# A chain of eight transformer stages on one core: each next stage's first statistics, normalizing and quantizing ahead of the last update of x

## What is computed

```
x = x + att0(layernorm(x), ctx)     # one head of 512, softmax, keys and values are the context and x itself
x = x + ffn0(layernorm(x))          # activations quantized to 8 bits per token, ternary weights, sigmoid gate
x = x + att1(layernorm(x), ctx)     # 16 heads, 4 key heads, rms norm and rotation of q and k, causal part
x = x + ffn1(layernorm(x))          # as ffn0, with silu and a Walsh-Hadamard transform of the hidden layer
x = x + att2(layernorm(x), ctx)     # linear attention with a gate
x = x + layer(layernorm(x))         # one ternary 512x512 product and a bias
x = x + att3(layernorm(x), ctx)     # x and output quantized to whole numbers, 16 heads of 32, softmax
x = x + ffn3(layernorm(x))          # weights interpolated (Catmull-Rom) from control points, silu gate
```

## Time and profile before

| | us |
|---|---|
| median of 3 runs | 2520.35 |
| lowest and highest run | 2519.28, 2526.17 |
| the profiled execution | 2523.76 |
| its span in the profile | 2521.9 |
| PE busy | 2291.3 (91%) |
| DVE busy | 1141.5 (45%) |
| ACT busy | 780.8 (31%) |
| POOL busy | 174.4 (7%) |

### The profile page before, as it was taken

How to read it: one execution, slowest core, us unless ns; L and a number is a source line. 1 busy time by engine, 2 the same in 40 slices (tenths; PEclk the granted TensorE clock), 3 DMA queues, 4 the chain that set the end, 5 groups by cost and what they waited for, 6 DMA issues and landing times.

```text
span 2521.9 us, 27455 instructions
## 1 busy us (share of the span) xinstructions
PE 2291.3 (91%) x10317; PEld 1328.8 (53%) x10340; DVE 1141.5 (45%) x2303; ACT 780.8 (31%) x1569; POOL 174.4 (7%) x356
## 2 busy tenths in 40 slices
PE   8998999999998969999999997968976888799999
PEld 3544544556664436666666664643433555444444
DVE  1432455364214835555555546844544666521111
ACT  1223322312222523333333324533332555311111
POOL 0000000000001211010010001100000000000000
PEclk9998999998999989999999999988988999899999
DMA  5442433434524210300000013010001111000000
GB/s 210 189 156 95 194 149 129 159 125 130 173 78 159 71 39 22 123 19 25 19 20 24 19 30 122 14 35 20 18 4 56 50 50 56 23 1 9 5 5 13
DMA packets 52519, 178.99 MB, mean 71 GB/s; under 512 B 5457, under 2 KB 25233, under 8 KB 46590
## 3 DMA queue, kind: packets, MB, share of 16 engines
q1 hardware_dynamic: 50662, 139.49, 16.1%
q0 software_dynamic: 1728, 37.75, 3.9%
HBM read 121.58 MB, written 46.47 MB: 67 GB/s over the span
## 4 chain that ended last, share of the span: by engine, by line
PE 72%; DVE 14%; ACT 6%; issue 5%; DMA 2%; POOL 1%; SPq 1%; DVEq 0%; ACTq 0%; POOLq 0%
PE psum L119 60%; PE psum L112 7%; PE psum L1438 4%; DVE small L2234 2%; DVE R L562 1%; ACT WK L2184 1%; ACT R L500 1%; PE psum L1040 1%; DVE R L1198 1%; DVE R L561 1%; PE psum L2152 1%; DVE R L1197 1%; DVE WK L242 1%; DVE small L1606 1%; DVE R L1755 0%
## 5 line engine op out<-in xcount | busy, mean ns | idle before, releaser
L119 PE MATMUL psum<-R,WK 128*125 128x512 f32 (+7 forms) x3458 | 1332.1, 531 | 30.0 <-DMA WK<-in_ctxT 7.4
L119 PEld LDWEIGHTS psum<-R,WK 128*112 128x112 f32 (+4 forms) x3472 | 583.2, 174 | 651.4 <-issue 531.1
L112 PE MATMUL psum<-small,WK 112*125 112x112 f32 (+6 forms) x2164 | 299.7, 269 | 150.2 <-ACT WK L2190 28.5
L112 PEld LDWEIGHTS psum<-small,WK 112*125 112x125 f32 (+6 forms) x2164 | 241.9, 155 | 252.4 <-issue 128.2
L119 PE MATMUL psum<-WK,R 128*112 128x375 f32 (+3 forms) x704 | 220.2, 451 | 13.1 <-DVE R L1755 8.9
L119 PE MATMUL psum<-WK 125*112 125x128 f32 (+3 forms) x1264 | 204.8, 299 | 1.5 <-DVE WK L890 1.2
L119 PEld LDWEIGHTS psum<-WK 125*112 125x112 f32 (+2 forms) x1264 | 165.7, 178 | 54.6 <-issue 43.7
L1606 DVE TENSOR_REDUCE small<-psum 112x1 f32<-112x487 f32 x128 | 84.9, 664 | 221.2 <-PE psum L119 219.4
L119 PE MATMUL psum<-R 128*128 128x112 f32 (+3 forms) x960 | 159.4, 310 | 28.0 <-DVE R L1755 22.8
L1528 ACT ACTIVATE WK<-psum,small 112x487 f32<-112x487 f32 x128 | 96.9, 757 | 259.1 <-DVE small L1608 258.4
L119 PEld LDWEIGHTS psum<-WK,R 128*112 128x112 f32 (+2 forms) x704 | 111.5, 170 | 86.7 <-issue 14.0
(11 more groups left out here) (212 smaller groups left out, 2041.2 us busy)
## 6 DMA issues: line engine op xcount, KB each, us to landing
R<-in_wf POOLq DMA_DIRECT2D x6, 4096.0 KB, 13.8
d_w<-R POOLq DMA_DIRECT2D x6, 2048.0 KB, 18.4
R<-d_w SPq DMA_DIRECT2D x6, 2048.0 KB, 14.7
WK<-in_ctxT SPq DMA_DIRECT2D x16, 750.0 KB, 5.5
d_v<-WK SPq DMA_DIRECT2D x16, 750.0 KB
R<-in_wq SPq DMA_DIRECT2D x7, 1024.0 KB, 7.7
R<-in_wo SPq DMA_DIRECT2D x6, 1024.0 KB, 16.7
d_k<-X SPq DMA_DIRECT2D x8, 750.0 KB, 3.2
```

The lines of the kernel that those rows point to most:

```text
L112: ins = pe.transpose(dst, src, idn[0:k, 0:k])
L119: ins = pe.matmul(dst, lhs, rhs, start=k == 0, stop=k == len(pairs) - 1)
```

## The change

`x_ready` loses its second form: it always waits for the last update, and it stands only where an engine touches what the old stage may still use. For PE that is behind the first transposes. ACT and POOL have none. Where x itself is needed, `x_back` waits for the copies of one batch.

Each stage has a new function `first(dve)`: the statistics, normalizing (and quantizing) of its first batch or tile, in the FFNs the statistics of the second tile too. The stage before calls it on DVE ahead of its own last update. `att1`'s tables are loaded at the start of `att0` and worked out there (`prepare`); `att2`'s bias and first two summaries are loaded with its weights during `att1` and `ffn1`; `layer`'s bias is loaded when `ffn1` is over; `att3`'s weights, biases and first keys and values are now all loaded when `att2` is over (the weights came sooner before). Tiles are placed so that these loads overwrite nothing.

```diff
         def x_ready(eng, n):
+            updates[n - 1].wait_drained(eng, TILES[n - 1] - 1, "y")
+
+        def x_back(eng, n, b=None):
             if n in (2, 4):
...
+                for i in range(NT):
+                    count = [at for at, _, _ in pieces(i)]
+                    if b is None or b in count:
+                        eng.wait_ge(sem(f"back{i}"), 16 * len(count) * (n // 2))
...
+        def ln_first(dve, n, xn, done):
+            x_back(dve, n, 0)
+            ln_stats(dve, dve_chain.on(dve), n, 0)
+            ln_apply(dve, n, 0, xn).then_inc(done, 1)
...
@@ context_part, dve @@
                         dve.tensor_reduce(wtot[:, b, 0:1], wsum[:, b, :], AX, ALU.add).then_inc(sem("context_sum"), 1)
+                        if b == 2:
+                            dve.wait_ge(sem("w2_threshold"), 1)
...
+                        elif b in (3, 4):
+                            quantize(dve, link, b - 3)
                         dve.wait_ge(sem("context_threshold"), b + 1)
...
@@ context_part, pool @@
                         pool.tensor_tensor(rk, ssp, neghalf[0:SP, :], ALU.pow).then_inc(sem("context_norms"), 1)
+                        if (b, s) == (2, 1):
+                            pool.wait_ge(sem("w2_abs"), 1)
+                            link(pool.partition_all_reduce(wtot[:, 6, 1:2], wsum[:, 6, 0:1], P, RADD))
...
-                    if b == 1:
-                        pool.wait_ge(sem("w2_abs"), 1)
...
@@ ternary_ffn @@
+            def first(dve):
+                stats(dve, 0)
+                quantize_x(dve, 0)
+                stats(dve, 1)
...
             def pe(pe):
-                x_ready(pe, n)
-                pe.wait_ge(sem(f"{stage}_weights"), 16 * (4 if hadamard else 3))
...
+                    for i, (b0, b1, b2, b3) in enumerate(iterations(4, NT)):
+                        if i == 2:
+                            x_ready(pe, n)
+                            pe.wait_ge(sem(f"{stage}_weights"), 16 * 3)
...
                         if b3 is not None:
+                            if b3 == NT - 1:
+                                stages[n + 1]["first"](dve)
                             update(b3)
...
@@ attention1 @@
             def sync(sp, load_next):
                 x_ready(sp, n)
+                x_back(sp, n)
...
@@ attention2, load @@
+                sp.dma_start(bg, io.bg2.to_broadcast([T, D])).then_inc(sem(f"{stage}_bias"), 16)
+                for b in range(2):
+                    load_kv(sp, b)
...
@@ attention3, dve @@
                         elif kind == "y":
                             out_ring.wait_filled(dve, b, "y")
+                            if b == NB - 1:
+                                stages[n + 1]["first"](dve)
                             link(dve.tensor_tensor(xr[:, b, :], xr[:, b, :], bp, ALU.add))
```

More of the change, by code:

```diff
@@ L201, in x_ready @@
         def x_ready(eng, n):
+            updates[n - 1].wait_drained(eng, TILES[n - 1] - 1, "y")
+        def x_back(eng, n, b=None):
             if n in (2, 4):
-                eng.wait_ge(sem(f"{'ffn0' if n == 2 else 'ffn1'}_back"), 16 * sum(len(list(pieces(i))) for i in range(NT)))
-            elif n:
-                updates[n - 1].wait_drained(eng, NB - 1, "y")
-            else:
-                raise ValueError(n)
+                for i in range(NT):
+                    count = [at for at, _, _ in pieces(i)]
+                    if b is None or b in count:
+                        eng.wait_ge(sem(f"back{i}"), 16 * len(count) * (n // 2))
         def context_stored(eng):
@@ L1244, in dve @@
                         if b3 is not None:
+                            if b3 == NT - 1:
+                                stages[n + 1]["first"](dve)
                             update(b3)
-                        if b0 is not None:
-                            quantize_x(b0)
+                        if b0:
+                            quantize_x(dve, b0)
                             if b0 + 1 < NT:
-                                stats(b0 + 1)
+                                stats(dve, b0 + 1)
                         if b2 is not None:
@@ L1285, in pool @@
                         h_scales(b2)
-            return dict(load=load, sync=sync, back=back, pe=pe, act=act, dve=dve, pool=pool)
+            return dict(load=load, sync=sync, back=back, first=first, pe=pe, act=act, dve=dve, pool=pool)
         def attention1(stage, n):
@@ L1301, in attention1 @@
             kTn = R.get(2 * NG * T, s=2, g=NG, t=T)
-            later = R.get(T, rows=T, dt=BF16)
+            later = Area(R1, 12160).get(T, rows=T, dt=BF16)
             W = Area(R0, 12288)
@@ L1558, in dve, with first @@
                     link(dve.tensor_tensor(c[:, 64:128], tmp[:, 64:128], cos, ALU.mult))
+            def first(dve):
+                ln_first(dve, n, xn, sem(f"{stage}_xn"))
+            def dve(dve):
+                x_ready(dve, n)
+                link = dve_chain.on(dve)
                 def four(v, a=0, z=P):
@@ L1935, in dve @@
                     if b3 is not None:
+                        if b3 == NB - 1:
+                            stages[n + 1]["first"](dve)
                         add_to_x(dve, dve_ring, b3)
@@ L2016, in dve @@
                     if b1 is not None:
+                        if b1 == 0:
+                            dve.wait_ge(sem(f"{stage}_bias"), 16)
+                        if b1 == NB - 1:
+                            stages[n + 1]["first"](dve)
                         link(dve.tensor_tensor(xr[:, b1, :], xr[:, b1, :], bias, ALU.add))
@@ L2099, in sync, with scale_of, normalized, whole_numbers @@
                                  ).then_inc(sem(f"{stage}_ctxV{b % 2}"), 16)
+            def scale_of(link, v, c):
+                dve = link.eng
+                link(dve.tensor_reduce(am, v, AX, ALU.max, apply_absolute_value=True))
+                link(dve.tensor_scalar(c, am, 1.0 / 127.0, 1e-8, ALU.mult, ALU.max))
+                link(dve.reciprocal(rr, c))
+                link(dve.tensor_scalar(v, v, rr, MAGIC, ALU.mult, ALU.add))
+            def normalized(dve, b):
+                link = dve_chain.on(dve)
+                link(ln_apply(dve, n, b, xn))
+                scale_of(link, xn, cx[:, b % 2:b % 2 + 1])
+            def whole_numbers(dve, b, name, v, vi):
+                if b:
+                    odd_ring.wait_filled(dve, b - 1, f"{name}T")
+                dve.tensor_scalar(vi, v, -MAGIC, 127.0, ALU.add, ALU.min).then_inc(sem(f"{stage}_{name}"), 1)
+            def first(dve):
+                ln_stats(dve, dve_chain.on(dve), n, 0)
+                normalized(dve, 0)
+                whole_numbers(dve, 0, "xi", xn, xi)
             def pe(pe):
-                x_ready(pe, n)
                 pe.wait_ge(sem(f"{stage}_weights"), 64)
@@ L2369, in act, with stats, first @@
                         drain(b0, "xnT", xnT)
+            def stats(dve, i):
+                dve.wait_ge(sem(f"{stage}_x{i % 2}"), arrived[i])
+                ln_stats(dve, dve_chain.on(dve), n, i, xf[i])
+            def first(dve):
+                stats(dve, 0)
+                ln_apply(dve, n, 0, xn, xf[0]).then_inc(sem(f"{stage}_xn"), 1)
             def dve(dve):
@@ L2434, in _ @@
                 if n == 4:
-                    x_ready(sp, n)
+                    stages[5]["load_bias"](sp)
                     spline["load"](sp)
-                stages[n]["sync"](sp)
+                if n == 6:
+                    x_ready(sp, n - 1)
+                    stages[n]["load"](sp)
+                if n != 5:
+                    stages[n]["sync"](sp)
             if upto < 8:
```

249 lines of the change are left out of this document (120 added, 129 removed).

## The result

| | before | changed |
|---|---|---|
| median of 4 runs, us | 2522.9 | 2440.58 |
| lowest and highest, us | 2519.28, 2526.17 | 2440.16, 2442.24 |
| the profiled execution, us | 2523.76 | 2440.16 |
| its span, us | 2521.9 | 2438.4 |

The ratio of the changed kernel to the one before is 0.9675, with a 95% interval from 0.9658 to 0.9692: 82 us or 3.3% less. The forecast was 2440.0 us. The two profiled executions lie 83.6 us apart, their spans 83.5.

A forecast was written before the change was run, and what follows sets the result against it. PE was taken to be busy nearly everywhere, so gains come only from its pauses and half clock. Terms summed to 80.3 us, taking the median from 2520.35 to 2440.0 us; range 2428 to 2460.

The forecast's parts named there:

- Prologue: Prologue: PE's 17.9 us wait behind POOL's W2 reduce and the quantizing waits go, with clock: 28.2 us, bounds 19.6 and 29.
- First FFN: Seam into the first FFN: DVE still waits for the copy of x, the last update follows; 0 us, bounds -1 and +1.
- Attention 1: Seam into attention 1: the 15.47 us pause goes, with half-clock loss; 18.6 us, first keys in time by 1.6 us.
- Attention 2: Seam into attention 2: pauses for x's way back and the bias go, 4.1 + 6.8 + 1.0 clock = 11.9 us.
- Layer, last FFN: Layer seam: only spline units' time remains, 3.9 us won. Last FFN seam: transposes sooner, product waits for update, 2.0 us won.
- Attention 3: Seam into attention 3: 1.1 us of the 8.8 us pause remain; 7.7 + 1.0 clock = 8.7 us, bounds 4 and 11.
- A stretched reduce: Prologue: quantizing beside POOL's all-reduce stretches it, so 5.8 and 2.8 us stay: 2448.6 us; 8%.
- `first` late at the second FFN and attention 3: At these two seams `first` is not reached before y is full; 4.6 us less won at each: 2449.2 us; 5%.
- First keys binding: Attention 1: first keys and values landing 7 us later cost 5.4 us: 2445.4 us; 5%.
- Seams that stay in part: Five later seams: waits the old barrier hid replace the pauses: 2473.6 us, or 2456.8 with half lost; 8%.
- More clock than counted: All seams win the 3.1 us of clock seen at attention 1: 2431.6 us; 9%.
- Slower by throttle: Long full stretches: without pauses the throttle grants less clock; 200 us more at half clock gives 2540 us; 2%.

The follow-up runs named there:

- The early copies: Changed kernel with the copies of the first FFN's tiles 0, 1 and 2 issued on SP ahead of the prologue's last four coefficient stores: 2432.18 us.
- the last FFN's early tile: Changed kernel with the last FFN's first statistics and normalizing ahead of the wait for attention 3's last y: 2437.25 us.
- the late order: Changed kernel with `first` put behind the last update of x on DVE again at all seven seams: 2464.5 us.
- the kernel with the barrier: Changed kernel with PE again waiting, from the first FFN on, for x's last update and all copies back at each stage's start: 2456.23 us.

## Why the prediction was right, point by point

| stretch | forecast | measured | of it pauses | of it clock |
|---|---|---|---|---|
| prologue | 28.2 | 30.6 | 25.0 | 5.6 |
| attention 0 | 0 | 2.7 | 0.0 | 2.7 |
| first FFN, from its seam | 0 | 1.7 | 1.1 | 0.6 |
| attention 1 | 18.6 | 18.8 | 15.4 | 3.4 |
| second FFN | 7.0 | 6.6 | 6.4 | 0.2 |
| attention 2 | 11.9 | 9.8 | 10.8 | -1.0 |
| layer | 3.9 | 3.8 | 3.1 | 0.7 |
| attention 3 | 8.7 | 7.2 | 7.9 | -0.7 |
| last FFN | 2.0 | 2.4 | 2.2 | 0.3 |
| sum | 80.3 | 83.5 | 71.8 | 11.7 |

Of the forecast's 80.3 us, 68.7 were pauses and 11.6 clock; measured are 71.8 and 11.7. The pauses are right in size and, but for one reason at attention 2, in mechanism. That the clock's sum agrees is luck: its four estimated terms (second FFN, attention 2, layer, attention 3) were 4.0 us and came out at -0.8, and 2.7 us in attention 0, for which the prediction had no term, and 1.1 more in the prologue made up for most of it. That the median came within 0.6 us of the forecast is partly luck too: the sum was 3 us short, and the median of the kernel before rose by 2.5 us with its fourth run.

**Prologue.** Right, shown alone by its own kernel (31.0 us). POOL's reduce needs its 10.9 us from whatever stands ahead of it, which the prediction had left open, and was through at 203.5 where 203 was counted. The quantizing was mis-sized a little: 10.1 us by its own kernel where 8.6 were counted. From the end of the product ahead of each pause to the end of the 40 rows behind it, the kernel before took 20.9 us (340.15 to 361.08) and 24.2 us (414.17 to 438.41), and the kernel with only the quantizing moved 17.6 both times: 3.3 us for the pause of 2.49, behind which PE also waited 0.52 us for ACT at full clock, and 6.6 us for the pause of 3.27, behind which half clock cost 3.4 us with the transposes and not 2.8. With that the 30.6 us of the stretch lie above the prediction's upper bound of 29.

**First FFN.** The 1.7 us of the stretch are more than the bound of 1, but the seam is as told: the pause stays, DVE blocks until 759.6, the last update follows, PE's product waits for it. The early copies show that the SP queue was the cause, as the prediction said: with the copies ahead of the stores the pause and 7.8 us of the stretch go.

**Attention 1.** Size and mechanism right. The slack for the first keys was counted too small: PE needed them at 874.39, and the last of them was issued at 862.69 with 1.74 us of its row, so with 6.1 us to land, an estimate from the earlier trace rows, they were there by 870.5, 3.9 us ahead. It was issued 8.2 us behind PE's last product, where it had been 12.1; the five table loads that are no longer ahead of it took 2.3 of that difference. What the 15.47 us pause was made of, the kernel before shows in SP's first table load and two rows of DVE:

```profile
893.54 0.34 SPq L1394 DMA_DIRECT2D WK<-in_cos  x1
...
900.10 0.22 DVE L1552 CAST R<-WK 112x112 bf16<-112x112 f32 x1 [9.85 <-DMA WK<-in_knw_row]
...
902.21 0.69 DVE L225 BATCH_NORM_STATS2 small<-X 112x6 f32<-112x512 f32 x1
```

From PE's end at 889.38 these are 4.2 us until the copies were back and SP could issue, 6.6 us for the five table loads, 2.1 us of table work and 2.6 us of statistics and normalizing until the transposes at 904.85. The experiments bring the parts back one at a time: 4.50 us of copies back, 4.52 us of tables (a part of them is covered when PE has work), 3.34 us of order on DVE, which is the last part and the 0.75 us of the update.

**Attention 2.** 10.8 us of pauses where 10.9 were counted, but of the two reasons given, "loaded a stage ahead" and "the DVE wait moves behind the g product", the second alone is enough. And the clock term had the wrong sign, 1.0 us gained forecast and 1.0 lost: the eight rows of the first product, from 1638.23 on, took 6.33 us, where the same rows, from 1710.42 on in the kernel before, took 5.37. So half clock did not go with the two long pauses; the short ones for the spline units are still ahead of these rows.

**Layer, last FFN.** Right within 0.5 us, the latter also in its parts: pauses of 2.50 and then 1.00 us, where the prediction had 2.5 and one more.

**Attention 3.** A pause of 0.69 us and a wait of 0.98 for the update where 1.1 in all were forecast. The clock term of 1.0 us was measured as -0.7.

**The rivals.** A stretched reduce: fallen. `first` late at the second FFN and attention 3: fallen, it waits for no y there; its tile is 0.6 us late at attention 3. First keys binding: fallen. Seams that stay in part: only the waits of under 1 us for the spline units at attention 2 and the layer, and the two for an update of 1 us each. More clock than counted: fallen, the four terms came out at -0.8 us in place of 12.4. Slower by throttle: no half clock appeared in attention 1 (1.00 in its stretch).

**How the parts share the gain.** Done alone in the kernel before, the prologue is worth 31.0 us; undone alone in the changed kernel, the order on DVE 23.9, the barrier on PE 15.7, the tables 4.0 (7.2 by the stretch in its trace), the early bias of attention 2 nothing: 75 of 82 us. They need not add up, since a late load hides behind a barrier. The waits for the biases of the layer and of attention 3 were not undone; what they hold by themselves stays open.

## What to carry to other kernels

At a seam, ask separately in which order the one engine works, what the common wait waits for, and where a load is waited for; where they stand in a row the pause is their sum, and each part can be read from the rows of the other queues inside the pause before anything is changed. Moving a wait to the instruction that uses the data can be enough, without moving the load a stage ahead. What stays behind after such a change is the seam that hangs on another queue: here SP, which issued the first tile's copies behind stores that nobody was waiting for yet.

## What the runs showed of the hardware that I had not expected

The same pauses do not always cost the same clock. Attention 0 is the same code in the same order in the changed kernel and in the experiments on it, and has the same 7.6 us of pauses, yet it took 194.3 us in the changed kernel and 196.8 in others. The same stretch of two of the kernels above (the last FFN's early tile; the late order):

```profile
562.09:756.92 194.83, 187.23 (x1057) 128.26 (x1056) 41.13 (x102) 43.32 (x66) 5.89 (x16) 0.98 0.37 120
```

```profile
562.08:758.78 196.70, 189.10 (x1057) 130.13 (x1056) 41.13 (x102) 43.30 (x66) 5.89 (x16) 0.97 0.36 119
```

PE's busy time is 187.2 or 189.1 us at a mean clock of 0.98 or 0.97, with nothing in this stage's code to tell them apart; the kernel with the barrier has 189.2. The kernel before has 196.9 us here, and with the prologue's edit alone 194.8. The second FFN spreads more: 149.8 us of PE's busy time in the changed kernel, 146.0 in the one with the last FFN's early tile, whose code is the same there. So the 2.7 us that attention 0 "won" can't be put down to the change, and a difference under some 4 us in one stage, or between two medians, is better read from the pauses than from the time. Why the clock differs, nothing here shows. POOL's reduce over the partitions was the other surprise: its own row is 0.40 us, but where POOL had something else to do until then it stood 10.87 us ahead of it and 6.75 behind (10.04 and 8.00 at the old place), though the sum that it waits for had been ready since 153.9, the end of ACT's last row for it. Where POOL had long been waiting for DVE, as at 288.82, the reduce began 0.14 us behind DVE's row, and only the stand behind it remained.
